# A top-p search that ends in a sorted list of 32 elements, and masks on both sides of a branch

## The reference, cut to what matters

```
def _adj_from_feats(Xa, W1, W2, W3):
    Q = Xa @ W1
    K = Xa @ W3
    logits = Q @ W2 @ K.T / TAU
    order = jnp.argsort(-logits, axis=1)
    vals = jnp.take_along_axis(logits, order, axis=1)
    probs = jax.nn.softmax(vals, axis=1)
    csum = jnp.cumsum(probs, axis=1)
    k_i = jnp.sum(csum < P_TOP, axis=1) + 1
    keep = jnp.arange(n)[None, :] < k_i[:, None]
    ...
    return jax.nn.softmax(masked, axis=1)
...
for s in range(STEPS):
    A = _adj_from_feats(Xa, W1, W2, W3)
    Xf = R @ Xf
    Xa = A @ Xa
    Z = Z + (Xf @ U1s[s] + Xa @ U2s[s])
```

## Time and profile before

| | us |
|---|---|
| median of 3 runs | 1350.34 |
| lowest, highest | 1349.93, 1350.79 |
| span of the profiled execution | 1347.3 |
| TensorE busy in it | 1193.1 |
| VectorE busy in it | 1089.4 |
| ScalarE busy in it | 573.3 |

### The profile page before, as it was taken

One profiled execution on the slowest core, in us unless ns is written; L12 is line 12 of the kernel. 1 busy time (PEld: TensorE's weight loads), 2 busy tenths in 40 slices (PEclk: granted clock), 3 DMA queues, 4 the chain that ended last, 5 costly groups with the idle time before them and its releaser, 6 DMA issues.

```text
span 1347.3 us, 17786 instructions
## 1 busy us (share of the span) xinstructions
PE 1193.1 (89%) x6042; PEld 587.6 (44%) x6042; DVE 1089.4 (81%) x1865; ACT 573.3 (43%) x1092; POOL 259.7 (19%) x236
## 2 busy tenths in 40 slices
PE   0578999999898997999995999898999999799893
PEld 0233555554343454554553554243454454354451
DVE  7887777753999899999899004999999899899778
ACT  2634454537422455554543437560462563231130
POOL 6032232321323011021021001321101111012011
PEclk9888999999999899999997999999999999899897
DMA  7136565632344000001000004236313313313364
GB/s 233 57 108 216 194 231 178 225 139 70 113 126 155 2 32 32 2 32 44 37 32 33 16 16 141 86 106 232 101 48 102 102 48 101 103 32 100 92 231 172
DMA packets 55774, 138.76 MB, mean 103 GB/s; under 512 B 9536, under 2 KB 9536, under 8 KB 51584
## 3 DMA queue, kind: packets, MB, share of 16 engines
q1 hardware_dynamic: 55680, 137.66, 30.6%
HBM read 88.10 MB, written 49.55 MB: 102 GB/s over the span
## 4 chain that ended last, share of the span: by engine, by line
DVE 58%; PE 23%; issue 9%; ACT 3%; DMA 3%; DVEq 1%; SPq 1%; POOL 0%; POOLq 0%; ACTq 0%
DVE WS L1499 20%; DVE w L1722 5%; PE UB L720 4%; DVE g L1582 4%; DVE E L1685 4%; DVE WS L1720 3%; PE AB L710 3%; PE AB L703 3%; DVE WS L1719 3%; PE RB L720 3%; PE XB L720 2%; PE AB L901 1%; DMA E<-adjT 1%; PE RB L901 1%; DMA Khl<-z_d 1%
## 5 line engine op out<-in xcount | busy, mean ns | idle before, releaser
L1499 DVE SCALAR_TENSOR_TENSOR WS<-E,g 128x2048 bf16<-128x2048 f32 x128 | 311.8, 2486 | 1.2
L1582 DVE TENSOR_REDUCE g<-E 128x1 f32<-128x2048 f32 x32 | 73.0, 2281 | 106.9 <-ACT E L1143 106.3
L1221 ACT ACTIVATE turns<-TB 128x512 f16<-128x512 f32 x128 | 75.6, 594 | 138.8 <-PE TB L735 138.8
L729 PE MATMUL TB<-ident,E 128*128 128x128 f32 x512 | 81.9, 289 | 40.0 <-DVEq L1787 38.8
L607 POOL TENSOR_TENSOR RT<-RT,AD 128x512 f32<-128x512 f32 x32 | 53.0, 1657 | 286.4 <-ACT RT L1197 285.3
L1685 DVE SCALAR_TENSOR_TENSOR E<-E,g 128x2048 f32<-128x2048 f32 x34 | 82.9, 2469 | 17.9 <-issue 17.2
L729 PEld LDWEIGHTS TB<-ident,E 128*128 128x128 f32 x512 | 66.8, 149 | 65.0 <-DVEq L1787 31.3
L1215 ACT ACTIVATE turns<-TB 128x512 f16<-128x512 f32 x128 | 75.6, 594 | 37.2 <-PE TB L729 37.1
L1143 ACT ACTIVATE E<-LB 128x512 f32<-128x512 f32 x128 | 75.7, 599 | 13.0 <-PE LB L810 11.7
L624 POOL TENSOR_TENSOR XHL<-WF,XHL 128x512 f16<-128x512 f32 x16 | 23.5, 1466 | 286.6 <-ACT XHL L1236 286.6
L1722 DVE MAX8 w<-WS 128x8 f32<-128x2048 f32 x32 | 73.4, 2295 | 1.1
(11 more groups left out here) (314 smaller groups left out, 2361.0 us busy)
## 6 DMA issues: line engine op xcount, KB each, us to landing
turns<-adj_parts SPq DMA_DIRECT2D x48, 512.0 KB, 3.8
E<-adjT SPq DMA_DIRECT2D x16, 1024.0 KB, 7.6
adj_parts<-turns SPq DMA_DIRECT2D x16, 1024.0 KB, 5.2
AH<-adj_parts SPq DMA_DIRECT2D x16, 512.0 KB, 4.0
z_d<-UO SPq DMA_DIRECT2D x31, 256.0 KB, 2.3
XR<-x SPq DMA_DIRECT2D x4, 1024.0 KB, 11.9
WS<-U SPq DMA_DIRECT2D x4, 1024.0 KB, 7.7
x_d<-E SPq DMA_DIRECT2D x16, 256.0 KB, 2.0
```

The source lines that it names most:

```text
L729: i = mm(bank[:, k * P:(k + 1) * P], src(k), ident32[:, :], is_transpose=True, start=(k == 0), stop=(k == KC - 1), skip_group_check=True)
L1221: a(ET[:, 1, c * KC:(c + 1) * KC, :].rearrange("p b c -> p (b c)"), TB[c % 2][:, :], ACT.Copy, scale=SE).then_inc(s_et, 1)
L1499: return v.scalar_tensor_tensor(junk[t % 2], e, g4[:, k, t:t + 1], e, op, ALU.mult, accum_out=g4[:, F_, t:t + 1])
L1582: ct(v.tensor_reduce(row(A2)[:, t:t + 1], E[:, slot, :], AX.X, ALU.max))
```

## The change

The search ends otherwise. SEARCH is (2, 3): after one counting round in step 0 and two in step 1, U is moved by formulas of its own (by_width from the spread, by_slope from the last two rounds), aimed at 14 elements above the threshold. The last round writes the elements below U to WS, sums them, and takes the eight largest of each of 16 parts of 128 columns (cand, 128 values a row). settle takes the 32 largest of these in order, eight at a time, with a match-and-replace that removes the eight found, runs the sum along the list with one scan instruction for all four tiles, and reads off the threshold. A row is flagged when the crossing isn't inside the list. The bracket, the subtraction, the flip and the old sums are gone.

Around the branch, AT_ONCE is 1: one tile is masked ahead of it and one directly behind the branch for the repairs; the next maxima follow, then the other two masks.

```
-SEARCH = (4, 4)
+SEARCH = (2, 3)
-AT_ONCE = 2
+AT_ONCE = 1
+AIM = ((14.0,), (9.0, 14.0))
+BEND, BELOW_BEND, LEAST = 0.4, 14.0, 0.3
+INERTIA, STEEP = 20.0, 3.0
+FEW, SHARP = 28.0, 1.05
+PARTS = 16
+PART = N // PARTS
+WIDE = 32
...
+            def by_width(ct, aim, last):
...
+                ct(v.tensor_tensor(row(D_), row(F_), row(TGT), ALU.subtract))
+                ct.free(v.tensor_copy(g4[:, UP:DP + 1, :], g4[:, U:D_ + 1, :]))
+                if last:
+                    few_left(ct)
+                ct(v.scalar_tensor_tensor(row(A1), row(U), aim, row(D_), ALU.mult, ALU.add))
+                ct.free(v.scalar_tensor_tensor(row(X_), row(A1), per_sig, row(RS), ALU.mult, ALU.mult))
...
+                ct(v.scalar_tensor_tensor(row(U), row(A1), 1.0, row(U), ALU.add, ALU.mult))
+                if last:
+                    capped(ct)
...
+            def by_slope(ct, aim):
...
+                ct.free(v.tensor_tensor(row(SU), row(U), row(UP), ALU.add))
+                ct.free(v.tensor_tensor(row(DU), row(U), row(UP), ALU.subtract))
...
+                ct(v.scalar_tensor_tensor(row(U), row(A1), 1.0, row(U), ALU.add, ALU.mult))
+                capped(ct)
...
-                for it in range(SEARCH_N):
+                for it in range(SEARCH_N - 1):
...
                         ct(s_of(E[:, slot, :], t, U, ALU.is_ge), behind=(1 if t < G - 1 else 0))
...
                     if it == 0:
...
+                        by_width(ct, AIM[s][0], SEARCH_N == 2)
+                    else:
+                        by_slope(ct, AIM[s][1])
+                for slot, t in tiles:
+                    ct(v.scalar_tensor_tensor(WS[:, :], E[:, slot, :], g4[:, U, t:t + 1], E[:, slot, :], ALU.is_lt,
+                                              ALU.mult, accum_out=g4[:, F_, t:t + 1]))
+                    for c in range(PARTS):
+                        i = v.max(cand[:, t, 8 * c:8 * c + 8], WS[:, c * PART:(c + 1) * PART])
+                    ct(i)
...
-                for slot, t in tiles:
-                    ct(v.tensor_scalar(WS[:, :], E[:, slot, :], g4[:, HI, t:t + 1], None, ALU.subtract))
-                    ct(v.tensor_scalar(bits(WS[:, :]), bits(WS[:, :]), bits(g4[:, FLIP, t:t + 1]), None,
-                                       ALU.bitwise_xor))
-                    ct(v.max(w8[:, t, :], WS[:, :]))
...
+                for k in range(WIDE // 8):
+                    for t in range(G):
+                        ct(v.max(win[:, t, 1 + 8 * k:9 + 8 * k], cand[:, t, :]), behind=G - 1)
+                    if k < WIDE // 8 - 1:
+                        for t in range(G):
+                            ct(v.match_replace(cand[:, t, :], win[:, t, 1 + 8 * k:9 + 8 * k], cand[:, t, :], 0.0),
+                               behind=G - 1)
+                dve.wait_ge(c_dve, ct.base + ct.n)
+                flat = (u[:, :, :].rearrange("p g k -> p (g k)") for u in (run, gate, win))
+                ct(v.tensor_tensor_scan(*flat, 0.0, ALU.mult, ALU.add))
+                ct(v.tensor_scalar(ge[:, :, :], run[:, :, :], 0.0, None, ALU.is_ge))
...
+                ct(v.scalar_tensor_tensor(flag[:, 1:5], row(BAD), WIN - 0.5, row(FULL), ALU.is_gt, ALU.max))
+                ct(v.scalar_tensor_tensor(flag[:, 5:9], row(BAD), 0.5, flag[:, 1:5], ALU.is_gt, ALU.max))
...
-                if g < NG - 1 and early(g + 1) < G:
-                    largest(g + 1, gq + 1, ct, slice(early(g + 1), G))
                 with dve.If(any_flag != NEVER):
                     for slot, t in tiles[AT_ONCE:]:
                         repaired(slot, t)
-                for slot, t in tiles[AT_ONCE:]:
+                slot, t = tiles[AT_ONCE]
+                masked(slot, t, THR).then_inc(s_kept, 1)
+                if g < NG - 1 and early(g + 1) < G:
+                    largest(g + 1, gq + 1, ct, slice(early(g + 1), G))
+                for slot, t in tiles[AT_ONCE + 1:]:
                     masked(slot, t, THR).then_inc(s_kept, 1)
```

More of the change, by code:

```diff
@@ L1624, in search @@
             def search(g, gq, ct):
                 tiles, sl = slots_of(g)
-                ct.free(v.memset(row(LO), 0.0))
-                ct.free(v.memset(row(HI), E_TOP))
                 if s == 0:
@@ L1723, in settle @@
-                ct(v.tensor_tensor(bits(h8[:, :, :]), bits(w8[:, :, :]), bits(many(FLIP)), ALU.bitwise_xor))
-                ct(v.tensor_tensor(pre[:, 0, :, 9:9 + WIN], h8[:, :, :], many(HI), ALU.add))
-                for k, (a, b) in enumerate(((0, 1), (1, 2), (2, 1), (1, 2))):
-                    ct(v.tensor_tensor(pre[:, b, :, 8:], pre[:, a, :, 8:],
-                                       pre[:, a, :, 8 - 2 ** k:9 + WIN - 2 ** k], ALU.add))
-                ct(v.tensor_scalar(ge[:, :, 1:], pre[:, 2, :, 9:], 0.0, None, ALU.is_ge))
@@ L1750, in settle @@
-                ct(v.tensor_tensor(row(A1), row(A1), h8[:, :, WIN - 1], ALU.max))
-                ct(v.scalar_tensor_tensor(row(A1), row(BAD), 1.5, row(A1), ALU.is_gt, ALU.mult))
-                ct(v.scalar_tensor_tensor(flag[:, 1:5], ge[:, :, WIN - 1], 0.0, row(A1), ALU.is_equal, ALU.max))
-                ct(v.scalar_tensor_tensor(flag[:, 5:9], row(BAD), 1.5, flag[:, 1:5], ALU.is_gt, ALU.max))
+                wide = [P, G, WIDE]
+                below = win[:, :, 1:]
+                ct.free(v.tensor_tensor(win[:, :, 0], row(DLO), row(F_), ALU.subtract))
@@ new lines, in settle @@
+                ct.free(v.tensor_reduce(row(FULL), cand[:, :, 7:8 * PARTS:8], AX.X, ALU.max))
+                for k in range(WIDE // 8):
[5 more added lines that the diff above has]
+                               behind=G - 1)
@@ new lines, in settle @@
+                dve.wait_ge(c_dve, ct.base + ct.n)
+                flat = (u[:, :, :].rearrange("p g k -> p (g k)") for u in (run, gate, win))
+                ct(v.tensor_tensor_scan(*flat, 0.0, ALU.mult, ALU.add))
+                ct(v.tensor_scalar(ge[:, :, :], run[:, :, :], 0.0, None, ALU.is_ge))
+                ct(v.tensor_tensor(run[:, :, 1:], ge[:, :, 1:], below, ALU.mult))
+                ct.free(v.tensor_tensor(row(FULL), row(FULL), win[:, :, WIDE], ALU.max))
+                ct(v.tensor_reduce(row(THR), run[:, :, 1:], AX.X, ALU.max))
@@ new lines, in settle @@
+                ct.free(v.tensor_tensor(run[:, :, 1:], below, row(THR).unsqueeze(2).broadcast_to(wide), ALU.is_equal))
+                ct(v.tensor_tensor(row(FULL), row(FULL), row(THR), ALU.is_ge))
+                ct(v.tensor_tensor(run[:, :, 1:], run[:, :, 1:], ge[:, :, 0:WIDE], ALU.mult))
+                ct.free(v.tensor_tensor(row(FULL), row(FULL), ge[:, :, 0], ALU.max))
+                ct(v.tensor_reduce(row(BAD), run[:, :, 1:], AX.X, ALU.add))
+                ct(v.scalar_tensor_tensor(flag[:, 1:5], row(BAD), WIN - 0.5, row(FULL), ALU.is_gt, ALU.max))
@@ L1754, in settle @@
+                ct(v.scalar_tensor_tensor(flag[:, 5:9], row(BAD), 0.5, flag[:, 1:5], ALU.is_gt, ALU.max))
+                ct.free(v.tensor_scalar(row(BAD), row(BAD), 1.0, None, ALU.add))
                 ct.free(v.scalar_tensor_tensor(row(SAFE), flag[:, 5:9], 0.0, row(THR), ALU.is_equal, ALU.mult))
```

121 lines of the change are left out of this document (46 added, 75 removed).

## The result

The changed kernel takes 1488.64 us (median of 4 runs, 1488.10 to 1490.32) against 1350.13 us for the kernel before beside it (4 runs, 1348.76 to 1350.79): 1.103 times the time, with a 95% interval of 1.101 to 1.106. The forecast was 1301 us, and the range ended at 1335. Rival (a), the missed row, had 1463 us and a chance of 0.19. The span of the profiled execution is 1488.4 us.

The account below looks back on a forecast made before the run. TensorE and VectorE were taken as nearly balanced, VectorE late at five of eight group starts. 1347.3 - 38.8 (waits) - 12.6 (clock) + 2 (gaps) = 1297.9; runs' median 3.0 higher, so 1301 us; range 1292 to 1335.

Parts of the forecast that it names:

- Rival (a): Row 610, first tile of step 1's group 1, misses the list; 42 halvings and repair, 197 us; 1463 us, chance 0.19.
- a row at the margin may lie on either side: At the list's edge: the float32 working's last digits aren't the chip's, so row 610 might not miss; no size.
- 13 more for the second tile: In (1,1), under (a): TensorE waits 13 us more because the second tile waits for the two other repairs.
- Waits for masked tiles: At five of eight group starts: TensorE's waits for VectorE's masked tiles all go, -38.8 us.
- VectorE's work: Over eight groups: VectorE loses 28 us per group in step 0 and 15 in step 1, 172 us in all.
- What VectorE has to spare in (1,3): Step 1, group 3: masked tile comes at 80.4 us, TensorE at about 94, leaving 13 us to spare.
- 0.4 us for each of the five starts: At the five waiting group starts: small TensorE gaps at ScalarE's copies show at full clock, 2 us in all.
- What is late next: At group starts: VectorE's shortened chain, 72.6 us in (1,3), is ready before TensorE, so all five waits go.
- The clock: At the five waiting starts: TensorE's 25.1 us busy at about half clock become about 12.6 at full clock, -12.6 us.
- Rival (b): VectorE stays the bound in some groups through small operations or jumps (MAX8 0.41 us and more); 1310 to 1340, chance 0.11.
- Rival (c): At TensorE's short gaps: the waits go but the low clock stays; 1313.5 us, chance 0.05.

Follow-up runs that it names:

- the kernel without the row: Changed kernel with the second aim of step 1 at 10 elements instead of 9, so no row falls outside the list: 1314.27 us, ratio 0.974.
- the last run above: Changed kernel, aim 10, old mask and maxima order; ScalarE's step 0 exponentials split into idle slots, copies at (0,0) and (1,1) reordered: 1300.32 us, ratio 0.9645.
- at twice 0.193: Changed kernel with aim 10 and each MAX8 over 128 columns issued twice, one result thrown away: 1324.79 us, ratio 0.982.

## Why the prediction was wrong, and what of it was right

**The step that failed is the weighing of rival (a).** The prediction had the row, the tile, the mechanism and a price within 26 us of what came. It gave the case 0.19 because the same working doesn't give the two repairs in order that the trace has. That was a reason to doubt ties, which hang on the last digit. Row 610 was outside by half an element. One weight of layer 0 rounded the other way took it inside, but then the working put a row of (0,2) outside: each version of the working had one repair. A repair should have been the forecast, with 1463 us. The runs showed 153.5 and 17.8 us of wait in this term's place, where the sum had nothing. The prediction's reading "a row at the margin may lie on either side" put the unknown of the chip's digits in place of a computed value.

**The terms of (a).** The halvings took 172 us instead of 163: one starts 4.10 us behind the last on average, not 3.9, and each turn of the loop has some 0.34 us with no instruction. The ranking took 21 us instead of 24. The whole repair was 205.4 us instead of 197 (+8), VectorE reached the branch at about 989, forecast 976 (+13), and TensorE was ready at 1040.9, forecast 1024.3 (-17): the errors nearly cancel, and the wait was 153.5 instead of 149. About half of the 25.6 us between 1463 and 1488.6 is the kernel without the row, which takes 1314 and not 1301; another 9 are the two waits, 171.3 us instead of 162. The "13 more for the second tile" is near the 17.8 measured, but its mechanism was wrong: the second tile's mask had next to nothing to do with it. It was the next maxima, whose move behind the second mask the prediction let pass at no cost.

**The forecast itself, with the row taken out.** Forecast 1297.9 us of span, measured 1313.8.
- Waits for masked tiles: -38.8 forecast, and none is left. Right.
- VectorE's work: -172 forecast, 1089.4 - 912.3 = -177 measured, busy 912 against "near 915". Right.
- What VectorE has to spare in (1,3): 13 us forecast. Its third counting pass of the first round began at 1148.71, its first mask ended at 1206.28, TensorE began at 1237.41: 31 us. The chain was 57.6 us, not 72.6. The sum charged it with the whole group's work, but two of the passes now lie ahead of the last exponentials.
- "0.4 us for each of the five starts": the term that was too small. 4.07 + 5.61 + 1.01 + 1.64 = 12.3 us where 2 stood, 10.3 more. The step "What is late next" was taken for VectorE's chain and not for ScalarE's list at the same starts, where exponentials of 4 us, and at (0,0) a copy that waits for GpSimd, stood ahead of the copies for TensorE. The row had the gaps only where VectorE's wait covered them.
- The clock: -12.6 forecast; TensorE's busy time fell by 1193.1 - 1185.0 = 8.1, 4.5 less than forecast. Two of the new waits have the lower clock behind them; but 2.1 of the 4.5 lie in the stretch ahead of (1,0), where TensorE was busy for 120.1 us against 118.0. There it waited 5.19 us for a DMA (4.42 before), and the sixteen products behind took 6.46 us (5.31 before, 3.63 at the higher clock). The prediction had no term for that stretch. With the 10.3 these are 14.8 of the 15.9 us.
- Where the waits and this stretch were mended, in the last run above, the two numbers came out: TensorE busy 1180.5 (-12.6), span 1297.1. That kernel has edits on ScalarE that the forecast didn't include, so it bears out the price of the clock and not the forecast.

**Rival (b)** was tied to MAX8 above 0.41 us; it measured 0.193 from start to start. But its bound was too high: at twice 0.193 the kernel already lost 10.5 us, by the way through the maxima. **Rival (c)** was right in kind and small: some low clock stayed in step 0, for another reason, the waits for ScalarE. That its 1313.5 us lies within 1 us of the 1314.3 without the row is chance: it kept the whole 12.6 us of the clock, and 10.3 of the real excess are waits.

**The small prices**, in the kernel with no missed row, on VectorE:

```profile
1172.60 3.19 DVE L1711 MAX8 cand<-WS 128x8 f32<-128x128 f32 x16
...
1193.73 0.08 DVE L1744 MATCH_VALUE_LOAD cand<-win,cand 128x8 f32 x1
1193.79 0.28 DVE L1744 MATCH_REPLACE8 cand<-win,cand 128x128 f32<-128x128 f32 x1
1193.98 0.09 DVE L1744 MATCH_VALUE_LOAD cand<-win,cand 128x8 f32 x1
...
1199.37 0.43 DVE L1748 TENSOR_TENSOR_SCAN run<-gate,win 128x132 f32<-128x132 f32 x1
```

64 parts are 12.8 us (forecast 13.4) by their 3.19 us for 16, and a replace with its load is 0.26 (forecast 0.33). One part alone lasts 0.28 us, near the 291 ns (an estimate) that the Trainium skill's formula for an fp32 tensor_tensor add gives (VectorE: DVE Perf Modes, section on the TRN2 errata). But issued without waits they start 0.193 us apart, and the 64 take 12.8 us and not its 18.6; here the measurement decides.

## What to carry to other kernels

A fast path with a slow fall-back has to be priced by its worst case in the data that the metric uses: where a working of the data says that one row falls back, that is the forecast, and a doubt about the last digits counts only for what hangs on them. An engine's time to spare is not one number: for each thing that others take from it (here masked tiles, the next maxima, the reciprocals) follow who waits for it, and what stands behind that waiting instruction in the waiting engine's own list. When a stall goes, read the list of every engine at that place, and put long instructions where their engine is idle, each by itself.

## What the runs showed of the hardware

- Small MAX8 on VectorE overlap: 0.28 us each over 128 columns, but 0.193 from start to start where none waits. The page's busy time leaves the overlap out: 102.2 us for 512 of them in the changed kernel, where 512 times the mean of 278 ns would be 142.
- The 42 turns of the loop on VectorE left 14.1 us without an instruction, 0.34 at each turn, and the branches with one mask ahead of them left VectorE idle for 24.0 us of "issue" in 7 places in the changed kernel.
- TensorE's first eight transposes took 1.97 us behind 153 us of waiting and behind 180, as much as behind the 4.67, 9.22 and 11.64 us of before. The granted clock was 0.50, the lower level, over these eight transposes of both, and over those at 440.87 of before. Behind 4.46 us of waiting they took 1.32, with a mean granted clock of 0.76.
